# Seeding the value bank from ScalarE in a one-core attention and feed-forward layer: the bias product leaves TensorE

## The chip, the cores and the metric

The kernel runs on one core of a Trainium2 chip. The metric is the device time of one launch in microseconds. TensorE (PE in the profile) multiplies matrices, ScalarE (ACT), VectorE (DVE) and GpSimd (POOL) work elementwise, SyncE (SP) issues most transfers. Each engine has its own instruction stream, kept in order, and the streams meet at semaphores only.

## The reference, cut to what matters

The input is 16 x 512 tokens of 256 numbers, 8192 tokens in all, in float32.

```
q = x @ Wq + bq;  k = x @ Wk + bk;  v = x @ Wv + bv
q, k = features(q), features(k)            # softmax over the 16 numbers of each head
context = (q k^T / (sum q + eps)) v        # 16 heads, no mask
x = layernorm(x + context @ Wo + bo)
h = silu(fp4(x) @ fp4(w_gate)^T) * (fp4(x) @ fp4(w_up)^T)     # 704 wide
out = layernorm(x + fp4(h) @ fp4(w_down)^T)
```

## The kernel before

Tokens go in 64 tiles of 128 (number `m`), four tiles to a sequence of 512 (`m = 4 i + t`, with `t` from 0 to 3). The program is a software pipeline that is written out by hand. Every engine has a function `attention(i, steps)` and a function `ffn(i, steps)`, which say for each step `t` what this engine does, for tiles of different age. `run` calls `attention` for all `i` first, then both in turn near the join (the feed-forward part begins at `i = 15`), then `ffn` alone. So the order on each engine is fixed, and a late instruction delays everything behind it.

A matrix product in float32 precision is made of three products each over two chunks of 128: high by high part, high by low part, low by high part. That gives six matmuls, all recorded at line L869. What a step of attention does, with the lines of the profile:

- TensorE: the output product of tile `m-7` into `wide` (six of 256 columns; before the q and k products for `t < 3`, behind them for `t = 3`). The q and k products of tile `m` into bank `pqk[m % 2]` (six of 512 columns). In `t = 0` two transposes of a feed-forward weight tile (L909). Then the values of tile `m` into bank `pv` (L917, the bias product, and six of 256 columns). In `t = 2` four matmuls that multiply the context by Wo (L926). Last the transposes of the q features (L937) and the k-v products (L939) of tile `m-2`.
- ScalarE: the copy of the values of tile `m-1` out of `pv` into `v_sb` (L524). In `t = 1` two operations on a weight tile (L528, L532). The high part of the q features (L518, behind the exponential and the seed in `t = 3`). The exponential of tile `m-1` (L543). The **seed** of tile `m+1` (L481): it writes the q and k biases, 512 columns, into `pqk`, and the q and k products add onto it. The high part of x of tile `m+2` (L478). The high part of the context product in `t = 2` (L554), of the weight tile in `t = 0` (L558). The squares of tile `m-8` (L502). From `m = 47` on also the first layer norm's last operation (L507), two tiles in each step until `m = 62`.
- VectorE: the low parts (L681 q features, L759 context product in `t = 2`, L752 weights), the maximum, the subtraction, the sum and the reciprocal of the features (L708, L733, L723, L739), the residual (L687) and the short layer norm operations from `m = 40` to 47 and from 56 to 63.
- GpSimd: the feature scaling (L384), the low part of x (L390), the output bias (L398) and weight operations (L402, L407, L412).

There is one `pv` bank. TensorE waits for the copy of tile `m-1` (semaphore `a_v`) before it begins tile `m`. In `pqk` the matmuls never begin a group, so that they add onto the seed; a product of `ident` and `mask` at the program's start (L876, semaphore `opened`) opens the banks for that. In `pv` the bias product begins the group: `ones_r` (ones in rows 0 and 32) by `bias_r` (the high part of the bias in row 0, the low part in row 32). VectorE makes `bias_r` at the start (L635 to L638), GpSimd clears both tiles (L367 to L371).

Of the kernel before, what the change touches and what calls it, by code (L numbers as in the profile page):

```python
# [22 lines left out]
F32 = mybir.dt.float32  # L23
F32R = mybir.dt.float32r
# [4 lines left out]
ALU = mybir.AluOpType  # L29
# [27 lines left out]
def layer_kernel(nc, x_tok, x_feat, Wq, bq, Wk, bk, Wv, bv, Wo, bo, w_ffn, I, out):  # L57
# [14 lines left out]
    with ExitStack() as ctx:  # L72
        def sb(name, shape, dt=F32):
            return ctx.enter_context(nc.sbuf_tensor(name, shape, dt))

        def sem(name):
            return ctx.enter_context(nc.semaphore(name))
# [14 lines left out]

        qkv_hi = sb("qkv_hi", [P, KC, 3 * D], F32R)
        qkv_lo = sb("qkv_lo", [P, KC, 3 * D], F32R)
        bias_b = sb("bias_b", [P, 2 * D])
        bias_r = sb("bias_r", [P, D], F32R)
        ones_r = sb("ones_r", [P, P], F32R)
        wo = sb("wo", [P, KC, D])
        bo_b = sb("bo_b", [P, D])

# [25 lines left out]
        def cube(a, b):  # L126
# [2 lines left out]

        w_qkv = part(KC * 3 * D).rearrange("p (c n) -> p c n", c=KC)  # L130
        xt_raw = [cube(KC, P) for _ in range(T)]
        bias_f = scratch[:, taken[0]:taken[0] + D]
        feat = [part(2 * D) for _ in range(2)]
        prob = [part(2 * NH * (HD + 1)).rearrange("p (h e) -> p h e", e=HD + 1) for _ in range(2)]
        v_sb = [part(D) for _ in range(2)]
# [65 lines left out]
        ld_xt = [sem(f"ld_xt{k}") for k in range(T)]  # L201
        ld_x = [sem(f"ld_x{k}") for k in range(T)]
        consts = sem("consts")
        wq_hi_s, wq_lo_s, bias_s, opened = sem("wq_hi_s"), sem("wq_lo_s"), sem("bias_s"), sem("opened")
        w_max, w_s2s, w_invs, w_scs, w_xns, w_ys, w_mgs, w_cs, w_gs, w_qs, w_t, w_his, w_los = (
            sem(f"w_{k}") for k in "max s2 inv sc xn y mg c g q t hi lo".split())
        a_xhi, a_xlo, a_xbo, a_seed, a_qk, a_qkv, a_max, a_sub, a_exp, a_v, a_sum, a_rec, a_feat = (
            sem(f"a_{k}") for k in "xhi xlo xbo seed qk qkv max sub exp v sum rec feat".split())
        a_post, a_qhi, a_qlo, a_kvm, a_c, a_chi, a_clo, a_out, a_res, a_sq, a_ln, a_x1 = (
            sem(f"a_{k}") for k in "post qhi qlo kvm c chi clo out res sq ln x1".split())  # L210
        e_max, e_s2s, e_invs, e_xns, e_ys, e_mgs, e_cs, e_gs, x_q = (
# [37 lines left out]
        def live_seq(i, ahead=0, count=NS):  # L249

            return not isinstance(i, int) or 0 <= i + ahead < count
# [41 lines left out]
        @block.sync  # L293
        def _(sp):
            def weights(k, w):
                sp.dma_start(w_qkv[:, :, k * D:(k + 1) * D],
                             w.rearrange("(c p) n -> p c n", p=P)).then_inc(ld_qkv[k], 16)

            def bias(k, b):
                sp.dma_start(bias_b[:, k * D:(k + 1) * D],  # L300
                             b.rearrange("(a n) -> a n", a=1).broadcast_to((P, D))).then_inc(ld_bias[0], 16)

            def loads(i, steps=range(T)):
                for t in steps:
                    m = T * i + t
                    if live(i, t):
                        need(sp, a_xhi, m - T + 1)
                        need(sp, a_xlo, m - T + 1)
                        sp.dma_start(xt_raw[t],
                                     x_feat.rearrange("(c p) n -> p c n", p=P)[:, :, bass.ds(m * P, P)]  # L310
                                     ).then_inc(ld_xt[t], 16)
                    if live(i, t, -6):
                        s = (t - 6) % T
                        need(sp, a_xbo, m - 6 - T + 1)
                        sp.dma_start(x_in[s], x_tok[bass.ds((m - 6) * P, P), :]).then_inc(ld_x[s], 16)

            loads(0, [0])
            weights(0, Wq)
            weights(1, Wk)
            bias(0, bq)  # L320
            bias(1, bk)
            weights(2, Wv)
            loads(0, [1])
            sp.dma_start(bias_f[0:33:32, :], bv.rearrange("(a n) -> a n", a=1).broadcast_to((2, D))
                         ).then_inc(ld_bias[1], 16)
            loads(0, [2])
            sp.dma_start(w_raw, w_ffn[0, :, :]).then_inc(ld_w, 16)
            loads(0, [3])
            sp.dma_start(wo[:, :, :], Wo.rearrange("(c p) n -> p c n", p=P)).then_inc(ld_wo, 16)
            sp.dma_start(bo_b[:, :], bo.rearrange("(a n) -> a n", a=1).broadcast_to((P, D))).then_inc(ld_wo, 16)  # L330
            for i in range(1, A_LOOP[0]):
                loads(i)
            for i in range(*A_LOOP):
                loads(i)
            for i in range(A_LOOP[1], NS + 2):
                loads(i)

            def stores(i):
                for t in range(T):
                    m = T * i + t  # L340
                    sp.wait_ge(y_o, m + 1)
                    sp.dma_start(out[bass.ds(m * P, P), :], o_t[t]).then_inc(st_out[t], 16)

            for i in range(0, NS):
                stores(i)
            for t in range(T):
                sp.wait_ge(st_out[t], 16 * NS)
# [3 lines left out]
        def _(pool):  # L351
# [11 lines left out]
                               pattern=[[0, KC], [HD, HB], [0, HD]], channel_multiplier=-1).then_inc(consts, 1)  # L363
            for b in range(2):
                pool.memset(prob[b][:, 0:NH, HD:], FEPS * FEPS / (1.0 + FEPS))
                pool.memset(prob[b][:, NH:, HD:], FEPS)
            pool.memset(bias_r[:, :].bitcast(F32), 0.0)  # L367
            pool.memset(ones_r[:, :].bitcast(F32), 0.0).then_inc(consts, 1)
            pool.wait_ge(consts, 6)
            pool.memset(ones_r[0:1, :].bitcast(F32), 1.0)  # L370
            pool.memset(ones_r[32:33, :].bitcast(F32), 1.0).then_inc(consts, 1)  # L371
            pool.wait_ge(consts, 7)

            pool.memset(hq[0][:, I:IP], 0.0)
            pool.memset(hq[1][:, I:IP], 0.0).then_inc(consts, 1)
# [92 lines left out]
        def _(act):  # L468
# [5 lines left out]
            def x_hi_step(n):  # L474
                s = n % T
                need(act, ld_xt[s], 16 * (n // T) + 16)
                need(act, a_qkv, n - T + 1)
                act.activation(xt_hi[s], xt_raw[s], ACT.Copy).then_inc(a_xhi, 1)  # L478

            def seed(n):  # L480
                act.activation(pqk[n % 2][:, :], bias_b[:, 0:2 * D], ACT.Copy).then_inc(a_seed, 1)  # L481

            x_hi_step(0)
            weights_hi(0)
            weights_hi(1)
# [4 lines left out]
            act.wait_ge(opened, 2)  # L490
            seed(1)
            x_hi_step(1)


            def squares(n, norm, added, sq):
# [14 lines left out]
            def attention(i, steps=range(T)):  # L510
                for t in steps:
# [9 lines left out]
                    if live(i, t, -1):  # L521
                        need(act, a_qkv, m)
                        need(act, a_post, m - 2)
                        act.activation(v_sb[b1], pv[:, 0:D], ACT.Copy).then_inc(a_v, 1)  # L524
                    if t == 1 and live_seq(i, 0, NW):
                        need(act, w_mgs, i)
                        need(act, w_xns, i + 1)
                        act.activation(w_y, w_xn, ACT.Square, scale=BOWL).then_inc(w_ys, 1)  # L528
                        need(act, w_cs, i)
                        need(act, w_gs, i)  # L530
                        need(act, w_ys, i + 1)
                        act.activation(w_mg, w_y, ACT.Copy, bias=FLOOR, scale=STEP).then_inc(w_mgs, 1)  # L532
# [93 lines left out]
        def _(dve):  # L626
            for k in range(3):
# [1 line left out]
                dve.wait_ge(wq_hi_s, k + 1)  # L629
                dve.tensor_tensor(qkv_lo[:, :, cols], w_qkv[:, :, cols], qkv_hi[:, :, cols].bitcast(F32),  # L630
                                  ALU.subtract).then_inc(wq_lo_s, 1)

            dve.wait_ge(consts, 6)
            dve.wait_ge(ld_bias[1], 16)
            dve.tensor_copy(bias_r[0:1, :], bias_f[0:1, :]).then_inc(bias_s, 1)  # L635
            dve.tensor_copy(bias_r[32:33, :], bias_f[32:33, :]).then_inc(bias_s, 1)
            dve.wait_ge(bias_s, 2)
            dve.tensor_tensor(bias_r[32:33, :], bias_f[32:33, :], bias_r[32:33, :].bitcast(F32),  # L638
                              ALU.subtract).then_inc(bias_s, 1)

            def layer_norm(k, g, batches, norm, done, sq):
                n, count, _ = batches[g]
# [220 lines left out]
        def _(pe):  # L863
# [10 lines left out]
            for b in range(2):  # L874
                for c in range(2):
                    last = pe.matmul(pqk[b][:, c * D:(c + 1) * D], ident[:, :], mask[:, :, :],  # L876
                                     start=c == 0, stop=True, skip_group_check=True)
                last.then_inc(opened, 1)
            pe.wait_ge(wq_lo_s, 2)

            def qkv(dst, t, lo, hi):
# [3 lines left out]
            def attention(i, steps=range(T)):  # L885
                for t in steps:
# [24 lines left out]
                    if live(i, t):  # L911
                        if isinstance(i, int) and (i, t) == (0, 0):
                            pe.wait_ge(wq_lo_s, 3)
                            pe.wait_ge(consts, 7)
                            pe.wait_ge(bias_s, 3)
                        need(pe, a_v, m)
                        pe.matmul(pv[:, 0:D], ones_r[:, :], bias_r[:, :], start=True, stop=False,  # L917
                                  skip_group_check=True)
                        qkv(pv[:, 0:D], t, 2 * D, 3 * D).then_inc(a_qkv, 1)
                    if t == 2 and live_seq(i, -1):  # L920
                        if isinstance(i, int) and i < A_LOOP[0]:
# [33 lines left out]
            def ffn(i, steps=range(T)):  # L955
                for t in steps:
# [8 lines left out]
                    if isinstance(i, int) and (i, t) == (0, 3):  # L965
                        pe.wait_ge(a_res, NT)
                        pe.wait_ge(a_clo, NS)
                        pe.wait_ge(w_los, NS)
                        pe.wait_ge(consts, 8)
                    if isinstance(i, int) and (i, t) == (1, 0):  # L970
                        pe.wait_ge(w_los, NW)
                    if live(i, t):
# [64 lines left out]
```

## Time and profile before

| | |
|---|---|
| median of 3 runs | 748.45 us (747.55 to 748.8) |
| the profiled execution, its own time | 746.88 us |
| its span | 745.0 us |
| busy: PE, DVE, ACT, POOL | 95%, 83%, 74%, 75% |
| L917, the bias product | 64 matmuls of 128x256 |
| attention alone | from the start to about 262 us |

Times of rows are counted from the span's start. Busy time is the union of an engine's instructions. The profiled execution's own time is its span and 1.9 us around it.

### The profile page before, as it was taken

What the parts mean: (1) busy time and instruction counts of PE and PEld (TensorE: products, weight loads), DVE (VectorE), ACT (ScalarE), POOL (GpSimd) and SP (SyncE); (2) the same over time, 40 slices, a digit from 0 to 9 for tenths busy, and PEclk for the clock granted to TensorE, in tenths of its full rate; (3) what the DMA queues carried; (4) which work ended last, traced back from release to release, by engine and by line L of the source; (5) the groups of instructions that cost most, each with busy time, mean ns of one, the idle gap of its engine ahead of it and who ended that gap; (6) DMA issues with size and microseconds to landing.
All of it is one profiled execution on the core that took longest, in us unless ns stands there. A gap on an engine that the chain in (4) does not pass through costs nothing.

```text
span 745.0 us, 16619 instructions
## 1 busy us (share of the span) xinstructions
PE 705.5 (95%) x4908; PEld 673.7 (90%) x4908; DVE 621.3 (83%) x1530; ACT 552.5 (74%) x1227; POOL 558.7 (75%) x585
## 2 busy tenths in 40 slices
PE   6999999999999978699999999999999999999984
PEld 5899999998888867699999999999999999999984
DVE  5988999899989976798788788787899887898784
ACT  5677777777899877467777777666666688788777
POOL 4677777776777686668878888788788788788761
PEclk9999999999999989899999999999999999999998
DMA  5222222222222110000000000000000011110114
GB/s 155 65 79 79 72 80 79 75 75 80 65 79 75 41 29 1 0 3 1 1 1 1 2 1 2 1 2 2 1 1 2 15 36 37 44 44 30 58 64 135
DMA packets 40045, 30.04 MB, mean 40 GB/s; under 512 B 3474, under 2 KB 39956, under 8 KB 39956
## 3 DMA queue, kind: packets, MB, share of 16 engines
q1 hardware_dynamic: 37508, 26.75, 12.0%
q10 hardware_dynamic: 2448, 2.23, 1.1%
q8 instruction: 40, 0.66, 0.4%
q14 instruction: 49, 0.40, 0.2%
HBM read 20.58 MB, written 8.39 MB: 39 GB/s over the span
## 4 chain that ended last, share of the span: by engine, by line
PE 81%; issue 6%; POOL 4%; DVE 4%; ACT 2%; DMA 1%; SPq 0%; ACTq 0%; POOLq 0%; DVEq 0%
PE bank L869 62%; PE wide L980 5%; PE wide L869 5%; PE bank L939 3%; PE bank L987 2%; PE bank L937 2%; PE wide L926 2%; POOL scratch L398 1%; POOL scratch L384 1%; PE bank L917 1%; DMA scratch<-L_attn_Wv 1%; POOL scratch L441 1%; ACT scratch L507 1%; DMA out<-scratch 1%; POOL scratch L407 0%
## 5 line engine op out<-in xcount | busy, mean ns | idle before, releaser
L869 PE MATMUL bank<-wf_hi,rounded 128*128 128x352 f32 (+1 forms) x1792 | 402.8, 310 | 12.7 <-DVE wf_lo L752 6.1
L869 PEld LDWEIGHTS bank<-wf_hi,rounded 128*128 128x128 f32 x1792 | 301.0, 190 | 15.4 <-DVE wf_lo L752 6.3
L869 PE MATMUL bank<-wf_lo,rounded 128*128 128x352 f32 (+1 forms) x896 | 274.2, 306 | 0.0
L869 PEld LDWEIGHTS bank<-wf_lo,rounded 128*128 128x128 f32 x896 | 170.7, 191 | 0.0
L441 POOL TENSOR_TENSOR scratch<-scratch 128x704 f32<-128x704 f32 x64 | 94.7, 1479 | 80.3 <-DVE scratch L825 76.6
L869 PE MATMUL bank<-qkv_hi,rounded 128*128 128x512 f32 (+1 forms) x512 | 147.5, 343 | 3.0 <-ACT bank L481 3.0
L869 PEld LDWEIGHTS bank<-qkv_hi,rounded 128*128 128x128 f32 x512 | 92.9, 190 | 13.7 <-issue 4.1
L426 POOL TENSOR_TENSOR scratch<-scratch 128x704 bf16<-128x704 f32 x64 | 99.4, 1553 | 7.7 <-ACT scratch L620 5.9
L390 POOL TENSOR_TENSOR rounded<-scratch,rounded 128x256 fp32r<-128x256 f32 x64 | 46.9, 734 | 60.8 <-ACT rounded L478 60.8
L794 DVE TENSOR_TENSOR scratch<-scratch,bank 128x352 f32<-128x352 f32 x64 | 33.2, 519 | 69.5 <-ACT scratch L581 67.2
L446 POOL TENSOR_TENSOR scratch<-scratch 128x704 f32<-128x704 bf16 x64 | 89.0, 1390 | 0.7 <-DVE scratch L829 0.7
L615 ACT ACTIVATE scratch<-scratch 128x704 uint8<-128x704 f32 x64 | 50.6, 791 | 49.4 <-POOL scratch L441 48.4
L869 PE MATMUL bank<-qkv_lo,rounded 128*128 128x512 f32 (+1 forms) x256 | 87.0, 340 | 0.0
L384 POOL TENSOR_TENSOR scratch<-scratch 128x512 f32<-128x512 f32 x64 | 68.0, 1062 | 11.7 <-DVE scratch L739 10.3
L869 PE MATMUL wide<-rounded 128*128 128x256 f32 x384 | 60.9, 295 | 6.3 <-issue 2.5
L839 DVE TENSOR_TENSOR rounded<-wide,rounded 128x768 fp32r<-128x768 f32 x64 | 61.0, 952 | 3.6 <-ACT rounded L599 3.0
L502 ACT ACTIVATE dump<-res,row_sum 128x256 f32<-128x256 f32 x128 | 63.8, 499 | 0.1
L869 PEld LDWEIGHTS wide<-rounded 128*128 128x128 f32 x384 | 51.1, 192 | 11.1 <-issue 6.6
L599 ACT ACTIVATE rounded<-wide 128x768 fp32r<-128x768 f32 x64 | 51.7, 808 | 9.6 <-PE wide L980 9.6
L980 PE MATMUL wide<-ident,scratch 128*128 128x128 f32 x384 | 52.4, 273 | 2.7 <-POOL scratch L446 2.7
L595 ACT ACTIVATE scratch<-bank 128x352 f32<-128x352 f32 x64 | 29.4, 459 | 32.0 <-PE bank L869 32.0
L581 ACT ACTIVATE scratch<-bank 128x352 f32<-128x352 f32 x64 | 29.6, 463 | 30.5 <-PE bank L869 30.5
(102 smaller groups left out, 1526.7 us busy)
## 6 DMA issues: line engine op xcount, KB each, us to landing
scratch<-x_feat SPq DMA_DIRECT2D x64, 128.0 KB, 2.2
scratch<-x_tok SPq DMA_DIRECT2D x64, 128.0 KB, 2.1
out<-scratch SPq DMA_DIRECT2D x64, 128.0 KB, 1.7
scratch<-w_ffn ACTq DMA_DIRECT2D x17, 128.0 KB, 2.2
scratch<-L_attn_Wq SPq DMA_DIRECT2D x1, 256.0 KB, 3.0
scratch<-L_attn_Wk SPq DMA_DIRECT2D x1, 256.0 KB, 3.2
scratch<-L_attn_Wv SPq DMA_DIRECT2D x1, 256.0 KB, 5.4
wo<-L_attn_Wo SPq DMA_DIRECT2D x1, 256.0 KB, 4.2
```

What stands on the lines that cost most here:

```text
L384: pool.tensor_tensor(heads(feat[b]), prob[b][:, :, 0:HD], over(hrec[b], 2 * NH, HD), ALU.mult).then_inc(a_feat, 1)
L390: pool.tensor_tensor(xt_lo[s], xt_raw[s], xt_hi[s].bitcast(F32), ALU.subtract).then_inc(a_xlo, 1)
L426: pool.tensor_tensor(hc[b], hxn[b], hmg[b], ALU.add).then_inc(h_c, 1)
L441: pool.tensor_tensor(blocks(hxn[b1]), blocks(hid[b1]), over(binv[b1], NB), ALU.mult).then_inc(h_xn, 1)
L446: pool.tensor_tensor(hq[b][:, 0:I].rearrange("p (a c e) -> p a c e", a=11, e=BLK), hg[b].rearrange("p (a c e) -> p a c e", a=11, e=BLK), b ...
L502: act.activation(dump[:, :], res[:, rows(n)], ACT.Square, bias=row_sum[:, at], scale=-1.0 * D, accum_out=row_sq[:, at]).then_inc(sq, 1)
L599: act.activation(hqt_hi[b1][:, :, :], wide[:, 0:IP].rearrange("p (c n) -> p c n", c=IC), ACT.Copy).then_inc(h_hi, 1)
L615: act.activation(hy[b1], hxn[b1], ACT.Square, scale=BOWL).then_inc(h_y, 1)
L794: dve.tensor_tensor(hid[b1][:, HALF:I], gated[1], pu[1][:, 0:HALF], ALU.mult).then_inc(h_b, 1)
L839: dve.tensor_tensor(hqt_lo[b1][:, :, :], wide[:, 0:IP].rearrange("p (c n) -> p c n", c=IC), hqt_hi[b1][:, :, :].bitcast(F32), ALU.subtract ...
L869: last = pe.matmul(dst, x(c), w(c), start=first and n == 0, stop=n == len(terms) - 1, skip_group_check=not first)
L980: last = pe.transpose(wide[:, c * P:(c + 1) * P], hq[b1][:, c * P:(c + 1) * P], ident[:, :])
```

## The change

The bias of the values takes the path that the biases of q and k have. The bias tile `bias_b` grows to three parts, the third is loaded by a broadcast transfer to all 128 rows (before: two rows, 2 KB). ScalarE gets a function `v_seed(n)`, which waits for the copy of tile `n-1` and writes the bias into `pv`. It runs once in the prologue and then in each step directly behind the copy L524. TensorE opens `pv` once, drops the 64 bias products, and waits for `a_vseed` in place of `a_v`. VectorE's three operations on `bias_r` and four memsets of GpSimd go.

```diff
             bias(1, bk)
             weights(2, Wv)
             loads(0, [1])
-            sp.dma_start(bias_f[0:33:32, :], bv.rearrange("(a n) -> a n", a=1).broadcast_to((2, D))
-                         ).then_inc(ld_bias[1], 16)
+            bias(2, bv)
             loads(0, [2])
...
+            def v_seed(n):
+                need(act, a_v, n)
+                act.activation(pv[:, 0:D], bias_b[:, 2 * D:3 * D], ACT.Copy).then_inc(a_vseed, 1)
+
             x_hi_step(0)
...
             seed(1)
             x_hi_step(1)
+            act.wait_ge(ld_bias[1], 16)
+            act.wait_ge(opened, 3)
+            v_seed(0)
...
                         act.activation(v_sb[b1], pv[:, 0:D], ACT.Copy).then_inc(a_v, 1)
+                        if m < NT:
+                            v_seed(m)
...
-            dve.wait_ge(consts, 6)
-            dve.wait_ge(ld_bias[1], 16)
-            dve.tensor_copy(bias_r[0:1, :], bias_f[0:1, :]).then_inc(bias_s, 1)
-            dve.tensor_copy(bias_r[32:33, :], bias_f[32:33, :]).then_inc(bias_s, 1)
-            dve.wait_ge(bias_s, 2)
-            dve.tensor_tensor(bias_r[32:33, :], bias_f[32:33, :], bias_r[32:33, :].bitcast(F32),
-                              ALU.subtract).then_inc(bias_s, 1)
...
+            pe.matmul(pv[:, 0:D], ident[:, :], mask[:, :, :], start=True, stop=True).then_inc(opened, 1)
...
-                            pe.wait_ge(consts, 7)
-                            pe.wait_ge(bias_s, 3)
-                        need(pe, a_v, m)
-                        pe.matmul(pv[:, 0:D], ones_r[:, :], bias_r[:, :], start=True, stop=False,
-                                  skip_group_check=True)
+                        need(pe, a_vseed, m + 1)
                         qkv(pv[:, 0:D], t, 2 * D, 3 * D).then_inc(a_qkv, 1)
```

ScalarE before, in steps `t = 2` and `t = 3` of a sequence from `i = 12` on. The bank of L524 is `pv`, that of L481 is `pqk`.

```order
L524 ACTIVATE scratch<-bank 128x256
L518 ACTIVATE rounded<-bank 128x256
L543 ACTIVATE scratch<-scratch 128x32x16
L481 ACTIVATE bank<-bias_b 128x512
L478 ACTIVATE rounded<-scratch 128x256
L554 ACTIVATE rounded<-wide 128x512
L502 ACTIVATE dump,row_sq<-res,row_sum 128x256
L507 ACTIVATE res<-res,nbias,rstd 128x256 x2
L524 ACTIVATE scratch<-bank 128x256
L543 ACTIVATE scratch<-scratch 128x32x16
L481 ACTIVATE bank<-bias_b 128x512
```

The same place in the changed kernel, where L522 is the former L524, L516 the former L518, L472 the former L481 and L476 the new operation.

```order
L522 ACTIVATE scratch<-bank 128x256
L476 ACTIVATE bank<-bias_b 128x256
L516 ACTIVATE rounded<-bank 128x256
L543 ACTIVATE scratch<-scratch 128x32x16
L472 ACTIVATE bank<-bias_b 128x512
L469 ACTIVATE rounded<-scratch 128x256
L554 ACTIVATE rounded<-wide 128x512
L500 ACTIVATE dump,row_sq<-res,row_sum 128x256
L505 ACTIVATE res<-res,nbias,rstd 128x256 x2
L522 ACTIVATE scratch<-bank 128x256
L476 ACTIVATE bank<-bias_b 128x256
L543 ACTIVATE scratch<-scratch 128x32x16
```

The new operation stands directly behind the copy out of the same bank, and everything else of the step moves behind it.

TensorE before, the end of the q and k products and the values of one tile.

```order
L869 MATMUL bank<-qkv_lo,rounded 128x512
L869 MATMUL bank<-qkv_hi,rounded 128x512
L917 MATMUL bank<-bias_r,ones_r 128x256
L869 MATMUL bank<-qkv_hi,rounded 128x256
L869 MATMUL bank<-qkv_lo,rounded 128x256
```

The same place in the changed kernel, where L861 is the former L869.

```order
L861 MATMUL bank<-qkv_lo,rounded 128x512
L861 MATMUL bank<-qkv_hi,rounded 128x512
L861 MATMUL bank<-qkv_hi,rounded 128x256
L861 MATMUL bank<-qkv_lo,rounded 128x256
```

One matmul of 256 columns and its weight load are gone from each tile.

## Rows read from the trace of the kernel before

**Rows 1.** Busy us of each engine in four stretches, then PE clock, DMA share, GB/s.

```profile
12.00:29.00 17.00, 15.52 (x98) 13.65 (x98) 14.72 (x34) 11.54 (x28) 9.58 (x12) 1.00 0.31 93
29.00:166.00 137.00, 136.77 (x926) 125.37 (x927) 124.31 (x317) 103.50 (x277) 102.60 (x132) 1.00 0.26 74
166.00:195.00 29.00, 27.55 (x183) 24.44 (x182) 27.70 (x74) 21.23 (x57) 19.35 (x26) 1.00 0.26 74
195.00:256.00 61.00, 59.55 (x400) 53.37 (x399) 55.16 (x148) 56.99 (x149) 44.65 (x58) 1.00 0.25 68
```

**Rows 2.** Line L917: durations in ns, first and last start in us.

```profile
L917 PE MATMUL bank<-bias_r,ones_r x64: 277/283/372, 12.2 to 259.0; 128*128 128x256 f32 x64
```

**Rows 3.** Timeline of PE: start, us, engine, line, [idle before <-releaser]; steady, then start.

```profile
124.61 0.28 PE L917 MATMUL bank<-bias_r,ones_r 128*128 128x256 f32 x1
124.73 0.28 PE L869 MATMUL bank<-qkv_hi,rounded 128*128 128x256 f32 x1
...
128.35 0.88 PE L869 MATMUL wide<-rounded 128*128 128x256 f32 x6
...
12.16 0.37 PE L917 MATMUL bank<-bias_r,ones_r 128*128 128x256 f32 x1 [0.48 <-DVE bias_r L638]
```

**Rows 4.** Timeline of ACT in the steady part, steps t = 0 and 1.

```profile
115.25 0.39 ACT L524 ACTIVATE scratch<-bank 128x256 f32<-128x256 f32 x1 [0.33 <-PE bank L939]
116.07 0.39 ACT L518 ACTIVATE rounded<-bank 128x256 fp32r<-128x256 f32 x1 [0.43 <-PE wide L869]
...
119.17 0.38 ACT L524 ACTIVATE scratch<-bank 128x256 f32<-128x256 f32 x1 [0.61 <-PE bank L939]
119.98 0.42 ACT L528 ACTIVATE scratch<-scratch 128x256 uint8<-128x256 f32 x1 [0.42 <-POOL scratch L407]
120.51 0.42 ACT L532 ACTIVATE scratch<-scratch 128x256 bf16<-128x256 uint8 x1
```

**Rows 5.** Timeline of DVE in the steady part, steps t = 1 and 2.

```profile
121.44 0.42 DVE L681 TENSOR_TENSOR rounded<-bank,rounded 128x256 fp32r<-128x256 f32 x1 [1.04 <-ACT rounded L518]
...
127.24 0.63 DVE L759 TENSOR_TENSOR rounded<-wide,rounded 128x512 fp32r<-128x512 f32 x1
```

**Rows 6.** Timeline of DVE and PE at step t = 3 of i = 11.

```profile
192.12 0.62 DVE L759 TENSOR_TENSOR rounded<-wide,rounded 128x512 fp32r<-128x512 f32 x1
...
192.84 0.95 PE L869 MATMUL wide<-rounded 128*128 128x256 f32 x6 [0.58 <-issue]
```

**Rows 7.** Timeline of ACT from i = 12 on, steps t = 0 to 3.

```profile
195.95 0.36 ACT L524 ACTIVATE scratch<-bank 128x256 f32<-128x256 f32 x1
196.32 0.39 ACT L518 ACTIVATE rounded<-bank 128x256 fp32r<-128x256 f32 x1
...
199.69 0.37 ACT L524 ACTIVATE scratch<-bank 128x256 f32<-128x256 f32 x1
200.23 0.42 ACT L528 ACTIVATE scratch<-scratch 128x256 uint8<-128x256 f32 x1 [0.17 <-POOL scratch L407]
...
204.38 0.36 ACT L524 ACTIVATE scratch<-bank 128x256 f32<-128x256 f32 x1
...
206.80 0.60 ACT L554 ACTIVATE rounded<-wide 128x512 fp32r<-128x512 f32 x1 [0.44 <-PE wide L926]
...
208.77 0.36 ACT L524 ACTIVATE scratch<-bank 128x256 f32<-128x256 f32 x1
209.03 0.62 ACT L543 ACTIVATE scratch<-scratch 128x512 f32<-128x512 f32 x1
209.55 0.59 ACT L481 ACTIVATE bank<-bias_b 128x512 f32<-128x512 f32 x1
```

**Rows 8.** PE's bias product at step t = 2 of i = 12.

```profile
204.87 0.32 PE L917 MATMUL bank<-bias_r,ones_r 128*128 128x256 f32 x1
```

**Rows 9.** Two late waits: ACT at i = 14, t = 3, and DVE at i = 15, t = 1.

```profile
242.83 0.38 ACT L518 ACTIVATE rounded<-bank 128x256 fp32r<-128x256 f32 x1 [0.32 <-PE wide L869]
...
250.64 0.42 DVE L681 TENSOR_TENSOR rounded<-bank,rounded 128x256 fp32r<-128x256 f32 x1 [0.89 <-ACT rounded L518]
```

More of the change, by code:

```diff
@@ L94, in layer_kernel @@
         qkv_lo = sb("qkv_lo", [P, KC, 3 * D], F32R)
-        bias_b = sb("bias_b", [P, 2 * D])
-        bias_r = sb("bias_r", [P, D], F32R)
-        ones_r = sb("ones_r", [P, P], F32R)
+        bias_b = sb("bias_b", [P, 3 * D])
         wo = sb("wo", [P, KC, D])
@@ L131, in layer_kernel @@
         xt_raw = [cube(KC, P) for _ in range(T)]
-        bias_f = scratch[:, taken[0]:taken[0] + D]
         feat = [part(2 * D) for _ in range(2)]
@@ L203, in layer_kernel @@
         consts = sem("consts")
-        wq_hi_s, wq_lo_s, bias_s, opened = sem("wq_hi_s"), sem("wq_lo_s"), sem("bias_s"), sem("opened")
+        wq_hi_s, wq_lo_s, opened = sem("wq_hi_s"), sem("wq_lo_s"), sem("opened")
         w_max, w_s2s, w_invs, w_scs, w_xns, w_ys, w_mgs, w_cs, w_gs, w_qs, w_t, w_his, w_los = (
             sem(f"w_{k}") for k in "max s2 inv sc xn y mg c g q t hi lo".split())
-        a_xhi, a_xlo, a_xbo, a_seed, a_qk, a_qkv, a_max, a_sub, a_exp, a_v, a_sum, a_rec, a_feat = (
-            sem(f"a_{k}") for k in "xhi xlo xbo seed qk qkv max sub exp v sum rec feat".split())
+        a_xhi, a_xlo, a_xbo, a_seed, a_vseed, a_qk, a_qkv, a_max, a_sub, a_exp, a_v, a_sum, a_rec, a_feat = (
+            sem(f"a_{k}") for k in "xhi xlo xbo seed vseed qk qkv max sub exp v sum rec feat".split())
         a_post, a_qhi, a_qlo, a_kvm, a_c, a_chi, a_clo, a_out, a_res, a_sq, a_ln, a_x1 = (
@@ L300, in bias @@
                 sp.dma_start(bias_b[:, k * D:(k + 1) * D],
-                             b.rearrange("(a n) -> a n", a=1).broadcast_to((P, D))).then_inc(ld_bias[0], 16)
+                             b.rearrange("(a n) -> a n", a=1).broadcast_to((P, D))).then_inc(ld_bias[k // 2], 16)
             def loads(i, steps=range(T)):
@@ L365, in _ @@
                 pool.memset(prob[b][:, 0:NH, HD:], FEPS * FEPS / (1.0 + FEPS))
[L366 to L372, printed above, removed]
+                last = pool.memset(prob[b][:, NH:, HD:], FEPS)
+            last.then_inc(consts, 1)
             pool.memset(hq[0][:, I:IP], 0.0)
@@ L968, in ffn @@
                         pe.wait_ge(w_los, NS)
-                        pe.wait_ge(consts, 8)
+                        pe.wait_ge(consts, 7)
                     if isinstance(i, int) and (i, t) == (1, 0):
```

## The prediction, made before the run

> **What bounds the kernel now.** I read the attention part first, since the change touches nothing behind it, and cut it by the busy times of the windows. From 29 to 166 us TensorE is busy for 136.77 of 137 us at the full granted clock (1.00, which is 2.4 GHz), and ScalarE for 103.50 [rows 1]. There every matmul less is time won. From 166 to 195 us the layer norm operations of VectorE join: it is busy for 27.70 of 29 us, and TensorE waits. From 195 to 256 us ScalarE is at 56.99 of 61 us, since it has two normalisations in each step. There TensorE's 59.55 us mislead: its gaps are few, but it is ScalarE that has hardly any room left. Then I read the timelines of the three engines, to see which wait ends last in each stretch.
>
> **What is removed.** 64 bias products go [rows 2]. Their recorded 283 ns overlap their neighbours. The price is the distance to the next matmul's start, 124.61 to 124.73, so 0.12 us [rows 3]. All 64 are worth 7.7 us, if TensorE is the bound at each.
>
> From tile 6 (29 us) to tile 39 (166 us) are 34 tiles: 34 x 0.12 = 4.1 us, if nothing else locks. Between 166 and 195 us it is mostly a VectorE chain that ends at the low part of the context product. That ends at 192.12 + 0.62 = 192.74, and TensorE's output product starts at 192.84, after 0.58 us without work [rows 6]. A faster TensorE waits longer there. I count one product of this stretch, 0.12 us, which stands behind such a wait and ahead of a ScalarE copy that VectorE waits for. **Gain: 4.2 us.**
>
> **What the new operation costs ScalarE.** `v_seed` waits for the copy's own end. Such a wait on one's own engine is to be seen at the weight operations: L528 ends at 119.98 + 0.42 = 120.40, L532 starts at 120.51, a gap of 0.11 [rows 4]. After a copy without such a wait the next operation starts 0.26 us behind its start (208.77 to 209.03) [rows 7]. So the copy's share grows from 0.26 to 0.36 + 0.11 = 0.47. The seed itself, 256 columns: a 512-column operation takes 0.52 us to the next one's start, a 256-column copy 0.26 [rows 7]; a read from SBUF is a little slower than one from PSUM, so 0.30. Sum: 0.21 + 0.30, about **0.50 us in each step**. Bounds: 0.26 if the wait cost nothing, 0.60 if the wait took twice its gap.
>
> The Trainium skill (ScalarE: Activation LUTs, What ACT_TABLE_LOAD costs) gives 186 ns + 0.833 ns per column for an activation with immediate scale and bias, and an overlap of 93 ns between neighbours. That is 399 ns for this one, where rows 4 and 7 have 0.36 to 0.39 us for 256 columns. By the page alone the addition would be 0.306 + 0.093 = 0.40 us, since the overlap is lost but no latency of the wait is counted. The loss below would be 3.3 us by it in place of 4.7, and the time 747.5 us.
>
> **Where ScalarE absorbs it: up to 195 us.** In `t = 0` the copy starts at 115.25 when TensorE lets it, and L518 at 116.07 waits for TensorE's output products. With the seed between: 115.25 + 0.39 + 0.11 + 0.30 = 116.05, just in time. In `t = 1`: 119.17 + 0.38 + 0.11 + 0.30 = 119.96, and L528 waits for GpSimd until 119.98 anyway [rows 4]. In `t = 2` and 3 ScalarE waits later in the step. So the cover is complete, but with 0.02 us to spare at two places. If `t = 1` loses its cover, L518 and VectorE's L681, which waits 1.04 us for it [rows 5], move as well.
>
> Who waits for L681: VectorE runs without a gap from 121.44 to the end of L759 at 127.87 [rows 5]. TensorE's output product of `t = 3` needs that, could start at 127.97 (with the 0.10 us of rows 6) and starts at 128.35 [rows 3]. The room is 0.38 us; three bias products less use 0.36 of it. So the 0.12 us for each tile hold, but nothing beyond.
>
> **Where it cannot: 195 to 256 us.** What one sequence grows by, from [rows 7]:
> - `t = 0`: the copy to L518 took 0.37 (195.95 to 196.32), and takes 0.36 + 0.11 + 0.30 = 0.77: +0.40.
> - `t = 1`: the copy to L528 took 0.54 with a wait of 0.17 for GpSimd, and takes 0.78: +0.23.
> - `t = 2`: here TensorE's values wait for the copy (204.38 + 0.36 = 204.74, product at 204.87 [rows 8]) and the context product L554 at 206.80 hangs on them. The seed ends at 204.38 + 0.47 + 0.37 = 205.22; TensorE starts at 205.35, 0.48 later, and has 0.14 less to do: +0.34. ScalarE's own work of the step, 0.50 longer with 0.44 of waiting taken, is hidden in that.
> - `t = 3`: nothing waits: +0.50.
>
> That is 1.47 us for a sequence. The stretch begins at `t = 0` of `i = 12`: 0.63 for its first two steps, then two full turns (2.93) to `t = 1` of `i = 14`, then 0.34 for `t = 2`, 0.18 for `t = 3` (0.50 less the 0.32 that L518 waits at 242.83), 0.40 and 0.23 to `t = 1` of `i = 15`. Sum **4.7 us**. It is handed on there: VectorE waits 0.89 us at 250.64 for ScalarE's L518 [rows 9], and from there on its chain has little room. Behind that the last seeds lie beside waits. The busy time as a check: 56.99 + 15.5 x 0.50 = 64.7 us of work for a stretch of 61, so at least 3.7 us more with all waits gone; with 0.30 each 61.6 us, so 0.6 us.
>
> **The start.** TensorE waited 0.48 us for the bias tile at 12.16 [rows 3]; that wait goes, and VectorE's three operations on the tile too. Against it the first copies get 0.50 us each on ScalarE, in a stretch in which TensorE is busy for only 15.52 of 17 us [rows 1], that is, others set the pace. I take 0, bounds -1.2 (the wait and six products) and +0.5. The bias transfer grows from 2 KB to 128 KB, but ScalarE asks for it only after its work on Wv, whose transfer stands ahead in the same queue; the third opening matmul runs while TensorE waits for its first operands. GpSimd's four memsets end before anyone needs them. All at nothing.
>
> **Sum.** -4.2 + 0 + 4.7 = +0.5 us. Against the profiled execution's 746.88 us that is 747.4; its own time is 1.6 us below the median of 748.45, to which the forecast goes: **748.9 us**. A measurement of this kernel can tell 0.2% or 1.5 us from no change, so this is no change that can be seen.
>
> **Rivals.**
> - **ScalarE has more room than I think** (0.22). With 0.30 us for the addition (the own wait nearly free), the steps grow by 0.20, 0.03, 0.14 and 0.30, and the waits at `t = 3` of `i = 14` take that one: about 2.0 us in the stretch. Then -4.2 + 2.0 = -2.2: 746.2 us. For it speaks that ScalarE still has 4 us idle; against it that in `t = 3` and at `t = 0` of these rows nothing but its own queue stands ahead of the next operation.
> - **The weight step loses its cover before 195 us** (0.25). From 29 to 166 us this is the end on the other side. If the seed in `t = 1` pushes L528 by 0.25 us in each of 8.5 sequences, VectorE's L681 and with it TensorE's output product move, since only 0.02 us of room is left there. That costs 2.1 us: +0.5 + 2.1, 751.0 us. It makes the kernel measurably slower from 0.12 us a sequence on (1.0 us over 8.5). For it speaks the 0.02 us; against it that L524 in `t = 1` starts by TensorE's clock and so 0.12 us earlier in the new order.
> - **TensorE's gain doesn't arrive** (0.06): the matmul behind takes over the bias product's start cost. Then the loss stands alone, 748.45 + 4.7 = 753.2 us. Against it: the starts are evenly 0.12 us apart.
> - **The clock** (0.02): TensorE's idle share from 195 to 256 us grows from 2% to some 14%. It was granted 1.00 in all four windows [rows 1]; at the lower level (1.2 GHz) for a tenth of the stretch it would lose some 6 us.
> - The balance as summed has the rest, 0.45.
>
> **How the numbers follow.** The range takes in 746.2 and 751.0: gain 3.2 to 5.4 with the start's bounds, loss 2.0 to 5.5, which makes -3.0 to +2.3, and the third rival's neighbourhood on the upper side: 745.9 to 751.8. Faster by over 0.2%: the first rival and a good start, 0.24. Slower: the second to fourth and a little of the balance's edge, 0.33. The rest is 0.43.
>
> **What would show it.** In the steady part of the new profile a sequence takes 0.48 us less than before, with TensorE still near 100% busy: right; only 0.2 us less and a wait of TensorE ahead of the output product of `t = 3`: the second rival. From the same sequence as before on, ScalarE near 100% busy and TensorE waiting for the seed in `t = 2`, sequences 1.5 us longer: right; under 0.7 us longer: the first rival. The copy to the seed 0.47 us and the seed to its successor 0.30 us, else the price is wrong. The feed-forward part should last as long as before. The prediction fails if the end of attention shifts by more than 1.5 us either way, most likely through the own wait's price, which enters 15 times.

## The result and the profile after

The changed kernel takes 751.72 us (median of 20 runs) against 749.51 for the kernel before (20 runs): ratio 1.0035, 95% interval 1.0026 to 1.0044, so 2.6 us slower (2.0 to 3.3). The prediction was 0.5 us slower and "no change that can be seen"; it is wrong. The time itself, 751.72 us, lies inside the stated range of 745.9 to 751.8, by 0.1 us. That is no merit of the sum: the median of the kernel before was 748.45 us in the three runs that the forecast started from and is 749.51 here, and the gain that the sum counted on did not come.

The profiled execution has a span of 749.3 us against 745.0. That of the kernel before was a quick one (746.88 us, 2.6 under the median of its 20 runs), so the two spans overstate the difference. Its windows, with the columns of [rows 1]:

```profile
12.00:29.00 17.00, 15.03 (x91) 12.77 (x90) 14.61 (x32) 14.33 (x36) 10.36 (x14) 1.00 0.32 94
29.00:166.00 137.00, 134.57 (x894) 121.71 (x893) 124.50 (x318) 115.54 (x311) 102.60 (x132) 1.00 0.26 74
166.00:195.00 29.00, 26.78 (x176) 23.48 (x175) 27.70 (x75) 23.57 (x63) 19.58 (x25) 1.00 0.27 74
195.00:256.00 61.00, 56.54 (x363) 48.60 (x362) 50.37 (x137) 58.84 (x156) 40.72 (x54) 1.00 0.23 66
```

From 29 to 166 us TensorE now idles for 2.4 us, where [rows 1] had 0.2. So the products that are gone did not shorten this part; they became idle time. From 195 to 256 us ScalarE is at 58.84 of 61 us, and VectorE fell from 55.16 to 50.37.

The turns say it better than the windows. A turn is the time from one Wo product of TensorE (L926, once in each sequence at `t = 2`; L915 in the changed kernel) to the next, read in the timeline. All times in us:

| kernel | ratio to before (95%) | L926 of i = 1 | i = 1 to 10 (nine turns) | usual turn there | i = 10 to 15 | 15 to 16 | from there to the end |
|---|---|---|---|---|---|---|---|
| before | 1 | 31.40 | 140.80 | 15.58 | 82.49 | 15.33 | 474.98 |
| changed | 1.0035 (1.0026 to 1.0044) | 30.09 | 141.04 | 15.65 | 86.91 | 14.46 | 476.80 |
| e1 product gone | 1.0005 (0.9993 to 1.0016) | 32.79 | 140.79 | 15.60 | 82.59 | 14.90 | 476.83 |
| e2 seed only | 1.0071 (1.0049 to 1.0092) | 32.15 | 141.13 | 15.66 | 87.09 | 14.35 | 476.48 |
| e3 before, L518 first | 0.9947 (0.9929 to 0.9964) | 34.23 | 139.32 | 15.48 | 80.45 | 14.85 | 475.35 |
| e4 changed, L518 first | 0.9980 (0.9968 to 0.9992) | 30.89 | 138.85 | 15.38 | 85.36 | 14.82 | 474.98 |
| e5 seed to tile 43 | 0.9985 (0.9973 to 0.9997) | 31.56 | 141.03 | 15.65 | 83.01 | 15.25 | 475.25 |
| e6 the same, L518 first | 0.9922 (0.9904 to 0.9940) | 30.74 | 139.57 | 15.39 | 80.63 | 15.06 | 475.10 |
| e7 seed placed later | 0.9972 (0.9958 to 0.9986) | 29.81 | 139.64 | 15.53 | 85.30 | 13.84 | 476.91 |
| e8 product gone, L518 first | 0.9897 (0.9877 to 0.9917) | 33.29 | 135.61 | 15.04 | 79.82 | 15.57 | 475.61 |

The last column varies between 475.0 and 476.9 us from execution to execution. The feed-forward part is the same in all ten, and e1, which seeds nothing, has 476.83. So I don't count the 1.8 us there as an effect. What is left of the profile's difference: -1.31 up to the first Wo product, +0.24, +4.42 and -0.87, together 2.5 us, beside the 2.6 us of the timed runs. So close a match is partly luck, since the first of these terms comes from one execution of each kernel and scatters by 1.8 to 2.8 us (see the start, below).

So of the forecast's three terms the late loss came (4.4 of 4.7 us), the start gained 1.3 instead of 0, and the gain of 4.2 us was not there at all. The experiments look for it.

### The profile page after: what moved, and what is told of

The parts are those of the page before. It is cut to its first block, busy times and chain, and to the rows that moved or that the text cites. A ratio compares the mean times of both kernels' runs of the same rounds, so it can differ in the third digit from the quotient of the medians.

```text
span 749.3 us, 16552 instructions
## 1 busy us (share of the span) xinstructions
PE 702.6 (94%) x4846; PEld 666.9 (89%) x4846; DVE 618.9 (83%) x1527; ACT 574.7 (77%) x1291; POOL 558.0 (74%) x581
## 4 chain that ended last, share of the span: by engine, by line
PE 55%; POOL 20%; issue 18%; DVE 3%; ACT 2%; DMA 1%; POOLq 0%; SPq 0%; ACTq 0%; DVEq 0%
PE bank L861 48%; POOL scratch L375 9%; POOL scratch L389 6%; PE wide L969 5%; PE bank L976 2%; POOL scratch L398 1%; POOL rounded L381 1%; POOL scratch L403 1%; POOL scratch L393 1%; DMA scratch<-L_attn_Wv 1%; POOL scratch L432 1%; POOL scratch L425 0%; POOLq L54 0%; DVE ln_t L653 0%; ACT scratch L505 0%
## 5 line engine op out<-in xcount | busy, mean ns | idle before, releaser
L861 PE MATMUL bank<-wf_hi,rounded 128*128 128x352 f32 (+1 forms) x1792 | 403.1, 310 | 12.8 <-DVE wf_lo L744 6.1
L861 PEld LDWEIGHTS bank<-wf_hi,rounded 128*128 128x128 f32 x1792 | 301.1, 190 | 15.3 <-DVE wf_lo L744 6.3
L861 PE MATMUL bank<-wf_lo,rounded 128*128 128x352 f32 (+1 forms) x896 | 274.3, 306 | 0.0
L861 PEld LDWEIGHTS bank<-wf_lo,rounded 128*128 128x128 f32 x896 | 170.7, 190 | 0.0
L861 PE MATMUL bank<-qkv_hi,rounded 128*128 128x512 f32 (+1 forms) x512 | 144.9, 345 | 4.6 <-ACT bank L472 3.2
L861 PEld LDWEIGHTS bank<-qkv_hi,rounded 128*128 128x128 f32 x512 | 92.1, 189 | 18.1 <-issue 4.2
L381 POOL TENSOR_TENSOR rounded<-scratch,rounded 128x256 fp32r<-128x256 f32 x64 | 46.9, 733 | 68.4 <-ACT rounded L469 68.4
L861 PE MATMUL bank<-qkv_lo,rounded 128*128 128x512 f32 (+1 forms) x256 | 86.5, 338 | 0.0
L861 PE MATMUL wide<-rounded 128*128 128x256 f32 x384 | 60.8, 294 | 10.9 <-DVE res L679 5.9
L861 PEld LDWEIGHTS wide<-rounded 128*128 128x128 f32 x384 | 50.9, 191 | 18.4 <-issue 14.3
```

The lines of the kernel that those rows point to most:

```text
L381: pool.tensor_tensor(xt_lo[s], xt_raw[s], xt_hi[s].bitcast(F32), ALU.subtract).then_inc(a_xlo, 1)
L861: last = pe.matmul(dst, x(c), w(c), start=first and n == 0, stop=n == len(terms) - 1, skip_group_check=not first)
```

## Where the gain went: a loop of four engines

In the changed kernel's steady part TensorE waits mainly at one place in each turn, ahead of the output product of `t = 0`. That product starts 0.87 us behind the four k-v products ahead of it, where 0.37 us is the distance without a wait. A smaller wait of 0.15 us stands ahead of the output product of `t = 2` (0.52 us). These are rows of its timeline in order of the dependence, `t = 0` first:

```profile
113.95 0.95 PE L861 MATMUL wide<-rounded 128*128 128x256 f32 x6 [0.28 <-DVE res L679]
115.00 0.39 ACT L516 ACTIVATE rounded<-bank 128x256 fp32r<-128x256 f32 x1 [0.43 <-PE wide L861]
116.32 0.41 ACT L469 ACTIVATE rounded<-scratch 128x256 fp32r<-128x256 f32 x1
116.80 0.74 POOL L381 TENSOR_TENSOR rounded<-scratch,rounded 128x256 fp32r<-128x256 f32 x1 [0.63 <-ACT rounded L469]
117.49 0.74 POOL L389 TENSOR_TENSOR scratch<-scratch,bo_b 128x256 f32<-128x256 f32 x1
118.18 0.64 POOL L398 TENSOR_TENSOR scratch<-scratch 128x256 f32<-128x256 f32 x1
118.91 0.42 ACT L528 ACTIVATE scratch<-scratch 128x256 uint8<-128x256 f32 x1
119.96 0.38 ACT L516 ACTIVATE rounded<-bank 128x256 fp32r<-128x256 f32 x1
120.38 0.42 DVE L673 TENSOR_TENSOR rounded<-bank,rounded 128x256 fp32r<-128x256 f32 x1 [1.05 <-ACT rounded L516]
```

L516, L469, L381, L389, L398, L673 and L679 are the former L518, L478, L390, L398, L407, L681 and L687. The reader can follow it: TensorE's output product of `t = 0` frees ScalarE, which after two more operations gives GpSimd its work; GpSimd's third operation frees ScalarE's weight operations of `t = 1`, behind which L518 stands; and that frees VectorE. From there VectorE has no gap until the residual of `t = 3`, L679 (129.04 to 129.45), for which the next turn's output product of `t = 0` waits. The values' products are not on this loop.

The kernel before had the same loop. There the profile put no wait on TensorE:

```profile
114.45 0.41 DVE L687 SCALAR_TENSOR_TENSOR res<-wide,scratch 128x256 f32<-128x256 f32 x1
...
114.54 0.61 PE L939 MATMUL bank<-scratch 128*128 128x128 f32 x4
...
115.02 0.95 PE L869 MATMUL wide<-rounded 128*128 128x256 f32 x6
...
122.06 0.61 PE L939 MATMUL bank<-scratch 128*128 128x128 f32 x4
...
122.43 0.96 PE L869 MATMUL wide<-rounded 128*128 128x256 f32 x6
```

At `t = 2` (122.43) the output product starts 0.37 us behind the start of the four products of L939, and so it does at `t = 1`; at `t = 0` (115.02) it is 0.48 us. The 0.11 us more are a wait for L687, which ends at 114.86, 0.16 us ahead of the product's start. In every steady turn of this kernel and of the changed one that product starts 0.15 to 0.16 us behind the residual's end, which is the sign that it waits for it. The record of the four L939 products runs to 115.15, past the start of the next one, so the wait leaves no idle time, and TensorE looked 100% busy. Round the loop: L518 of `t = 0` at 116.07 [rows 4] to L681 at 121.44 [rows 5] is 5.37 us, and from the end of L687 to L518 1.21 us; the rest of the turn is VectorE's 9.0 us. Together 15.58. The sum has to be the turn, since the points lie one turn apart; what makes it a loop is that no stretch of it has room.

## The experiments

**e1.** The TensorE half alone: the bias is left out, so the output lacks it.

```diff
-                        pe.matmul(pv[:, 0:D], ones_r[:, :], bias_r[:, :], start=True, stop=False,
-                                  skip_group_check=True)
-                        qkv(pv[:, 0:D], t, 2 * D, 3 * D).then_inc(a_qkv, 1)
+                        qkv(pv[:, 0:D], t, 2 * D, 3 * D, first=True).then_inc(a_qkv, 1)
```

> This kernel leaves the value bias out: the 64 bias products go, nothing takes their place, and the start stays as before. Loop theory (a chain through four engines, VectorE's steps t = 1 to t = 3, TensorE's output product of t = 0, ScalarE, GpSimd and ScalarE's L518 of t = 1, sets 15.58 us a sequence up to 166 us, not TensorE): a sequence there stays at 15.55 to 15.60 us, TensorE shows a wait of 0.2 to 0.3 us ahead of the output product of t = 0, and the whole gains at most 1.5 us, from the start and from places where TensorE is the bound. TensorE theory (that of the prediction): sequences of 15.1 us, the whole 4 to 5 us faster.

Measured: ratio 1.0005 (0.9993 to 1.0016), turns of 15.60 us, and this row in its timeline:

```profile
116.54 0.95 PE L869 MATMUL wide<-rounded 128*128 128x256 f32 x6 [0.23 <-DVE res L687]
```

Taking 64 products away brings this kernel nothing that can be measured, even with nothing put in their place. The wait stands where the loop theory puts it. TensorE as the bound is refuted.

**e2.** The ScalarE half alone: the products stay, and ScalarE writes the bank ahead of them.

```diff
+            def v_seed(n):
+                need(act, a_v, n)
+                act.activation(pv[:, 0:D], bias_b[:, 0:D], ACT.Copy).then_inc(a_vseed, 1)
...
+                        if m < NT:
+                            v_seed(m)
...
-                        need(pe, a_v, m)
+                        need(pe, a_vseed, m + 1)
```

> The bias products stay and also begin the group as before; ScalarE additionally writes 256 columns into the value bank behind each copy, at the place of the change, and TensorE waits for that. The written values are overwritten by the product, so the output is the reference's. It is the ScalarE half of the change alone. Both theories: from the L926 of i = 10 to that of i = 15 some 4.4 to 4.9 us more than the 82.5 us of before, since ScalarE has no room there. Loop theory: the steady part stays within 0.1 us a sequence of 15.58; the whole is 4 to 6 us slower, so that the whole change differs from this by little. TensorE theory: the same loss in the late stretch, and the changed kernel would have to be 4 us faster than this one.

Measured: 1.0071 (1.0049 to 1.0092), 5.3 us slower; from `i = 10` to 15 87.09 us, 4.60 more than before; steady turns 15.66. The late loss is the seed's alone, and up to 166 us the seed is hidden. The changed kernel is some 2.7 us better than this one, where the expectation had little. It has the same turns, so I put that down to the start (below). The two intervals together leave some 1.7 us of doubt on the 2.7, so the times alone would not refute the 4 us of the TensorE theory; the turns do.

**e3 and e4.** The loop opened, in the kernel before and in the changed one: in `t = 1` L518 goes ahead of the weight operations.

```diff
-                    if t < 3 and live(i, t, -3):
+                    if t in (0, 2) and live(i, t, -3):
                         q_hi()
...
+                    if t == 1 and live(i, t, -3):
+                        q_hi()
                     if t == 1 and live_seq(i, 0, NW):
                         need(act, w_mgs, i)
                         need(act, w_xns, i + 1)
```

> The kernel before, with one move: in t = 1 ScalarE does L518 (high part of the q features) ahead of the two weight operations that wait for GpSimd. This opens the supposed four-engine loop, since VectorE's L681 of t = 1 no longer waits for GpSimd's L407. Loop theory: VectorE's wait of 1.04 us goes, TensorE's own work of 15.47 us becomes the bound, a sequence falls from 15.58 to 15.45 to 15.50 us, about 1 us over the steady part, and up to 1 us more behind 166 us. TensorE theory: nothing changes up to 166 us, since TensorE is the bound there already.

> The changed kernel with the same move of L518. Loop theory: now the missing bias products pay, a sequence falls from 15.66 to 15.0 to 15.2 us, 4 to 6 us over the steady part; the late loss of 4.4 us stays in the main, so the whole ends 1.5 to 4 us faster than the kernel before. TensorE theory and any theory by which the products were free: the sequence stays above 15.5 us and the whole stays slower than before.

Measured, e3: 0.9947 (0.9929 to 0.9964), 4.0 us faster. Each steady turn is 15.48 us; a turn that TensorE alone sets should be 15.58 - 0.11 = 15.47. The output product of `t = 0` now starts 0.37 us behind the k-v products in all nine turns: the hidden wait is gone. Moving one operation past two others, without taking any work away, gave what 64 matmuls less did not. Its timeline at `t = 1`:

```profile
121.54 0.39 ACT L518 ACTIVATE rounded<-bank 128x256 fp32r<-128x256 f32 x1 [0.33 <-PE wide L871]
121.82 0.41 ACT L530 ACTIVATE scratch<-scratch 128x256 uint8<-128x256 f32 x1
```

L518 no longer stands behind L530 (the former L528). The gain behind 166 us was 2.0 us, twice what I allowed.

Measured, e4: 0.9980 (0.9968 to 0.9992), 1.5 us faster than before. The turn fell from 15.65 to 15.38 us only, above the 15.0 to 15.2 expected. It has a second loop, and its rows show it, `t = 0` to 3:

```profile
113.54 0.95 PE L863 MATMUL wide<-rounded 128*128 128x256 f32 x6 [0.45 <-DVE res L681]
117.57 0.39 ACT L522 ACTIVATE scratch<-bank 128x256 f32<-128x256 f32 x1 [0.49 <-PE bank L930]
117.99 0.39 ACT L476 ACTIVATE bank<-bias_b 128x256 f32<-128x256 f32 x1
...
121.42 0.36 ACT L522 ACTIVATE scratch<-bank 128x256 f32<-128x256 f32 x1
121.81 0.39 ACT L476 ACTIVATE bank<-bias_b 128x256 f32<-128x256 f32 x1
122.13 0.37 ACT L516 ACTIVATE rounded<-bank 128x256 fp32r<-128x256 f32 x1
122.53 0.42 DVE L675 TENSOR_TENSOR rounded<-bank,rounded 128x256 fp32r<-128x256 f32 x1 [0.45 <-ACT rounded L516]
...
128.37 0.41 DVE L681 SCALAR_TENSOR_TENSOR res<-wide,scratch 128x256 f32<-128x256 f32 x1
```

From 117.57 to 122.50 ScalarE has no gap, with two seeds in it; VectorE waits for its L516 of `t = 2`, and TensorE for VectorE. So with the first loop open the seeds do cost something in the steady part. The output product of `t = 0` stands 0.78 us behind the k-v products, a wait of 0.41 us.

**e8.** e1 and e3 together: no bias, no seed, loop open.

> The kernel that leaves the value bias out (no product, no seed), with L518 first. Loop theory: with the loop opened and no seed on ScalarE the 0.48 us of four products pay in full or nearly so: steady turns of 15.0 to 15.15 us against 15.48 with the products, some 3 to 4 us faster over the whole than that kernel. If TensorE's saving can't be had for another reason (the next matmul takes over the cost), turns stay at 15.4 us or more.

Measured: 0.9897 (0.9877 to 0.9917), 7.7 us faster than before, turns of 15.04 us. Against e3 that is 0.44 us for four products. The timeline shows that TensorE isn't quite the only bound here: the output product of `t = 0` stands 0.43 us behind the k-v products, and again 0.15 to 0.16 us behind the residual's end, so 0.06 us of each turn is a wait. Which path closes this loop I did not trace. Without the wait TensorE's own turn is 14.98 us, and e4 (15.38 - 0.41) and e7 (15.53 - 0.55) give 14.97 and 14.98. Against 15.48 that is 0.12 us for each product: the price of [rows 3] was right, for a TensorE that is the bound. The nine steady turns gain 3.71 us against e3, and the whole kernel 3.7 us by the times. With this order of the rest, a cheaper place for the bias should bring no more than that.

**e5 and e6.** Seeds for tiles 0 to 43 only; from 44 on the bias product is back. e5 is made from the changed kernel, e6 from e4.

```diff
-                        if m < NT:
+                        if m < SEEDED:
                             v_seed(m)
...
-                        need(pe, a_vseed, m + 1)
+                        if m < SEEDED:
+                            need(pe, a_vseed, m + 1)
+                        else:
...
+                            need(pe, a_v, m)
+                            pe.matmul(pv[:, 0:D], ones_r[:, :], bias_r[:, :], start=True, stop=False,
+                                      skip_group_check=True)
```

> The changed kernel, but only tiles 0 to 43 are seeded by ScalarE; from tile 44 on the bias product is back on TensorE (its tiles are made in the steady part in place of the start), and ScalarE writes nothing there. If the late stretch makes the whole loss, as the loop theory says: the four turns from i = 10 to 15 fall back from 86.9 to 82.5 us, the steady turns stay at 15.66, and the whole is within 0.2% of the kernel before, about 4 us under the changed one by profile. If the seeds cost in the steady part too, it stays over 0.2% slower than before.

> The same with L518 ahead of the weight operations in t = 1. Loop theory: steady turns of 15.38 us as in the changed kernel with that move, late turns as in the kernel before with that move, so 0.5 to 1.5 us faster than the latter, at a ratio of about 0.993 to the kernel before. TensorE theory has no expectation of its own left here; if the two halves were to act on each other, the ratio would lie above 0.995.

Measured, e5: 0.9985 (0.9973 to 0.9997), 83.01 us from `i = 10` to 15: 3.9 of the 4.4 us lost are back. So the last 20 seeds make most of the loss; 0.5 us more than in the kernel before stay, with a cause that was not looked for. With steady and late turns as before or a little longer, it is still 1.1 us faster than the kernel before (0.2 to 2.0). I put that down to the new start, though this execution's first Wo product, at 31.56, doesn't show it. Measured, e6: 0.9922 (0.9904 to 0.9940), steady turns of 15.39, late ones as in e3. Both kernels make the bias tile on VectorE at `i = 5`; in e6 the two turns there are 16.43 and 15.02 us, 0.7 us more than two usual ones, in e5 0.1 us. It is the fastest kernel with the reference's output, 5.8 us under the kernel before; the interval overlaps that of e3, so what the first 44 seeds add to e3's move is not settled by the times.

**e7.** e4 with the seed moved in three of four steps so that it doesn't wait for the copy just ahead: behind L518 in `t = 1` and 2, behind the exponential in `t = 3`. In `t = 0` it stays behind the copy.

```diff
-                        if m < NT:
-                            v_seed(m)
+                    if t == 0 and live(i, t, -1) and m < NT:
+                        v_seed(m)
...
+                    if t == 1 and live(i, t, -1) and m < NT:
+                        v_seed(m)
...
+                    if t == 3 and live(i, t, -1) and m < NT:
+                        v_seed(m)
```

> The changed kernel with L518 first, and the seed of the values moved: behind L518 in t = 1 and 2 and behind the exponential in t = 3, so that it no longer waits for the end of the copy just ahead of it. If the wait on ScalarE's own copy costs some 0.15 us in three of four steps, a late turn falls from 17.38 to 16.9 to 17.0 us and a steady turn, whose remaining loop runs over ScalarE's t = 1 and 2 and VectorE, from 15.38 to 15.1 to 15.25; the whole 2 to 4 us faster than with the seed behind the copy. If only the 0.30 us of the seed itself count, less than 0.5 us.

Measured: 0.9972 (0.9958 to 0.9986), 0.6 us better than e4 with overlapping intervals. The expectation missed. Late turns fell by 0.16 us (17.38 to 17.22), not 0.4 to 0.5, and steady turns grew from 15.38 to 15.53. The own wait did go, but in `t = 1` the exponential (L549 there) comes later and VectorE's sum waits for it:

```profile
119.78 0.72 DVE L723 TENSOR_REDUCE scratch<-scratch 128x32 f32<-128x544 f32 x1 [0.23 <-ACT scratch L549]
```

In the late stretch TensorE now waits longer for the seed: 5.0 us of idle time against 3.1 in e4. This is its view of waits from 195 to 256 us (total us, times, longest):

```profile
PEld bank L869 <- ACT bank L476: 8.7, 10, 1.3
...
PE bank L869 <- ACT bank L476: 5.0, 7, 0.9
```

## Why the prediction was wrong, point by point

**The step that failed** is the gain: "34 x 0.12 = 4.1 us, if nothing else locks", and behind it "There every matmul less is time won". It rested on TensorE's busy time, 136.77 of 137 us [rows 1], which hid a wait of 0.11 us a turn. I did look for a lock: "Who waits for L681". I followed VectorE's chain to L759 and TensorE's output product of `t = 3`, found 0.38 us of room, and stopped. VectorE has no gap behind L759 either. Some operations later stands L687, and the output product of `t = 0` waits for it with no room at all. e1 shows the products worth nothing in this order, e3 and e8 that the loop was the reason. The third rival, "TensorE's gain doesn't arrive" (0.06), had the right outcome for a wrong cause: the price of a product was right, 0.12 us (e8).

**The cover in the steady part** was right: with the seed, turns are 15.65 us in the changed kernel and 15.66 in e2, against 15.58. The second rival's 0.25 us a turn did not come; VectorE's L673 waits 1.05 us as before. The stretch that holds the seeds, from L516 of `t = 0` to L673 of `t = 1`, is 5.38 us against 5.37; the 0.07 us by which the turn grew lie in VectorE's gapless stretch, 9.07 us against 9.00.

**ScalarE's price** was 0.50 us and measured a little less. In the changed kernel's late stretch, `t = 2`:

```profile
221.45 0.36 ACT L522 ACTIVATE scratch<-bank 128x256 f32<-128x256 f32 x1
221.84 0.39 ACT L476 ACTIVATE bank<-bias_b 128x256 f32<-128x256 f32 x1
222.16 0.37 ACT L516 ACTIVATE rounded<-bank 128x256 fp32r<-128x256 f32 x1
```

Copy to seed 0.39, seed to next 0.32, together 0.71 where it was 0.26 to 0.27: 0.44 to 0.45 more. The estimate by the figures of the Trainium skill (ScalarE: Activation LUTs, What ACT_TABLE_LOAD costs) was 0.40; the trace lies between page and forecast.

**The late loss**, forecast 4.7 us, was 4.42 us by the turns from `i = 10` to 15, of which 0.87 us came back in the turn behind, where ScalarE has only one more seed. I had called that part even. The two full turns from `i = 12` to 14 grew by 1.21 and 1.26 us, where 1.47 was forecast. With the measured 0.44 us in place of 0.50 the forecast's four steps add up to 1.23, so the price explains most of the difference. The places were right: TensorE waits for the seed in `t = 2`.

```profile
222.28 0.39 PE L861 MATMUL bank<-qkv_hi,rounded 128*128 128x256 f32 x1 [0.27 <-ACT bank L476]
```

**The start** was mis-sized: 0 forecast, with bounds of -1.2 to +0.5. The profile of the changed kernel has 1.3 us gained, and e5's time is 1.1 us shorter (0.2 to 2.0) though its turns are 0.7 us longer in all, which makes an estimated 1.8 us. VectorE's three operations on the bias stood ahead of its first work for tile 0. That much is shown: tile 0's first maximum starts 3.5 us behind the start of VectorE's last weight operation in the five kernels that make the bias tile there, and 1.8 to 2.3 us in the five others. In this profile TensorE begins tile 0's values at 10.97 in place of 12.16 [rows 3]:

```profile
10.97 0.36 PE L861 MATMUL bank<-qkv_hi,rounded 128*128 128x256 f32 x1 [0.30 <-ACT bank L476]
```

I had weighed the 0.48 us of visible wait, and not that the whole chain of the first tiles moves with it. What becomes of it until the first Wo product is less certain: the Wo product of `i = 1` lies at 29.8 to 31.6 us in the five kernels with the new start (mean 30.6) and at 31.4 to 34.2 in the five with the old one (mean 32.8), with a scatter inside each group whose cause I did not test.

**The sum.** +0.24 + 4.42 - 0.87 - 1.31 = 2.5 us, where the forecast had -4.2 + 0 + 4.7 = 0.5. The missing gain of 4.2 us alone would have made it 4.7; that the result was only 2.6 us is the unforeseen gain of the start and the turn behind `i = 15`, so the forecast came as near as it did by luck. The range's working was off too: its gain of 3.2 is 3.7 by the start's bounds, its -3.0 is 2.0 - 5.4 = -3.4, and its lower end of 745.9 follows from neither.

## What to carry to other kernels

An engine that the profile shows 100% busy is the bound only if no chain of waits closes round it and sets the period. Compare the distance between like instructions in all steps: a step in which one starts 0.1 us later than in the others has a wait that busy time hides. And follow a gapless engine to the end of the turn, past the first consumer that has room, before a saving is booked. Then look for the order that opens the loop: here one operation moved past two gave 4 us, and only then did a matmul less count.

Work that moves from one engine to another should be priced in each stretch by itself. In the changed kernel the first 44 seeds cost almost nothing in the turns, and the last 20 about 4 us. With L518 first the split by tile (e6) beats seeding all tiles (e4); whether it beats seeding none (e3) the times don't settle.

## What the runs showed of the hardware that I had not expected

- A ScalarE operation that waits for its predecessor's end starts 0.03 us behind that end after a copy out of PSUM (221.45 + 0.36 to 221.84), where the weight operations have 0.11 us (120.40 to 120.51 [rows 4]). So such a wait costs 0.13 us here (0.39 against 0.26 from the copy's start to the next), not 0.21.
- TensorE's recorded busy time read 105.00 of 105 us from 50 to 155 us both in e3, with turns of 15.48 us, and in e8, with 0.5 us less work and a small wait in each turn of 15.04 us. It can't tell how much room is left.
